# Attention scores from two fp32r parts in 64-row halves, with TensorE's order in a group written out by hand

## What is computed

```
qkv = x @ w_attn.T;  q, k = rope(q), rope(k)
scores = q @ k.T / sqrt(16), masked above the diagonal
y = softmax(scores) @ v + gating * softmax(q @ ak.T / sqrt(512)) @ av
x = layernorm(x + y @ w_proj.T)
base = x @ base_w.T + base_b;  res = x @ A.T;  probs = softmax(x @ router_w.T)
combine = top-2 of probs, normalised
x = layernorm(x + base + 0.5 * sum_e combine_e * (res @ B_e.T))
```

## Time and profile before

| | |
|---|---|
| median of 3 runs | 961.23 us (957.89 to 962.98) |
| profiled execution, its own time | 958.21 us |
| its span in the trace | 956.5 us |
| TensorE busy | 885.7 us, 93% of the span |
| VectorE busy | 737.3 us, 77% |
| ScalarE busy | 496.7 us, 52% |
| stage A, about | 0 to 233 us |
| stage B, about | 233 to 699 us |
| stage C, about | 699 to 956 us |

### The profile page before, as it was taken

The page is one execution under the profiler, slowest core; times in us unless marked ns, Lnnn a source line. Parts: engine busy times, 40 slices in busy tenths (PEclk is TensorE's granted clock), DMA queues, the critical chain, the costliest instruction groups (busy, mean ns, idle before and its releaser), DMA issues.

```text
span 956.5 us, 16144 instructions
## 1 busy us (share of the span) xinstructions
PE 885.7 (93%) x5420; PEld 493.3 (52%) x5420; DVE 737.3 (77%) x2225; ACT 496.7 (52%) x1052; POOL 259.3 (27%) x285
## 2 busy tenths in 40 slices
PE   5999999886999999999999999999978999999996
PEld 4878787561223222332222333222357888888884
DVE  4676757769898889888889988887555777767766
ACT  4243434232777777777777788778751122121210
POOL 0324334222232322332322332223331221212211
PEclk9999999985999999999999999999989999999999
DMA  7224143316555433455533455436110101011010
GB/s 248 55 68 121 56 122 98 95 30 134 101 99 101 100 62 61 81 100 101 94 60 62 87 100 100 86 63 180 47 34 1 36 31 44 22 44 35 31 34 33
DMA packets 50410, 73.11 MB, mean 76 GB/s; under 512 B 8996, under 2 KB 21540, under 8 KB 50340
## 3 DMA queue, kind: packets, MB, share of 16 engines
q1 hardware_dynamic: 49828, 71.43, 32.4%
q10 hardware_dynamic: 512, 0.79, 0.3%
HBM read 55.12 MB, written 16.78 MB: 75 GB/s over the span
## 4 chain that ended last, share of the span: by engine, by line
PE 78%; DVE 12%; ACT 6%; issue 2%; DMA 1%; POOL 1%; SPq 0%; DVEq 0%; ACTq 0%
PE bank L1328 17%; PE bank L1427 15%; PE bank L1338 10%; PE bank L385 10%; PE bank L386 9%; PE bank L387 9%; PE bank L1528 4%; ACT pt L790 3%; PE bank L1409 1%; DVE xl L872 1%; DVE xtl L1058 1%; ACT xth L815 1%; DVE asb L933 1%; DVE asum L936 1%; ACT asb L694 1%
## 5 line engine op out<-in xcount | busy, mean ns | idle before, releaser
L790 ACT ACTIVATE pt<-bank 128x512 f32<-128x512 f32 (+3 forms) x768 | 334.1, 493 | 96.3 <-PE bank L1328 88.7
L955 DVE CUSTOM_DVE_ANT_0 bank<-bank,cmask 128x512 f32<-128x512 f32 (+3 forms) x512 | 234.8, 523 | 24.5 <-PE bank L1338 22.7
L1328 PE MATMUL bank<-qs,ks 98*128 98x512 bf16 (+3 forms) x768 | 208.1, 335 | 19.0 <-ACT pt L790 18.9
L958 DVE TENSOR_REDUCE mx<-bank 128x1 f32<-128x512 f32 x256 | 163.4, 685 | 31.8 <-PE bank L1338 31.6
L620 POOL TENSOR_SCALAR_AFFINE_SELECT pt<-pt 128x512 f32<-128x512 f32 x128 | 83.6, 653 | 327.8 <-ACT pt L790 327.8
L1427 PE MATMUL bank<-pt,vb 128*32 128x512 f32 (+3 forms) x1536 | 164.5, 500 | 0.9 <-POOL pt L620 0.9
L1328 PEld LDWEIGHTS bank<-qs,ks 98*128 98x128 bf16 x768 | 57.8, 97 | 179.2 <-ACT pt L790 131.6
L1338 PE MATMUL bank<-km,qm 48*128 48x512 bf16 (+3 forms) x768 | 124.0, 340 | 11.4 <-DVE mx L955 7.8
L1338 PEld LDWEIGHTS bank<-km,qm 48*128 48x128 bf16 x768 | 32.6, 94 | 119.6 <-DVE mx L958 42.2
L815 ACT CAST xth<-bank 128x512 fp32r<-128x512 f32 x16 | 9.4, 586 | 146.2 <-PE bank L1502 146.2
L955 DVE DVE_READ_ACCUMULATOR2_ANT mx<- 128x1 f32 x512 | 72.3, 141 | 0.0
(11 more groups left out here) (152 smaller groups left out, 1435.6 us busy)
## 6 DMA issues: line engine op xcount, KB each, us to landing
qs<-q_parts SPq DMA_DIRECT2D x32, 256.0 KB
q_parts<-part SPq DMA_DIRECT2D x48, 128.0 KB, 2.4
k_parts<-part SPq DMA_DIRECT2D x48, 128.0 KB, 2.4
ks<-k_parts SPq DMA_DIRECT2D x16, 384.0 KB
qs<-q_parts SPq DMA_DIRECT2D x32, 128.0 KB
ks<-k_parts SPq DMA_DIRECT2D x16, 256.0 KB
qm<-in_x SPq DMA_DIRECT2D x16, 256.0 KB, 2.7
out<-outb SPq DMA_DIRECT2D x16, 256.0 KB, 2.0
```

The source lines that it names most:

```text
L790: act.activation(pt[k % PT_BUFS][:, h, 0:width(st)], half(n % SCORE_BUFS)[:, 0:width(st)], ACT.Exp, scale=float(HD) ** -0.5).then_inc(S("e ...
L955: last = ve.tensor_tensor_reduce(blk, blk, cmask[:, BANK - nk * P:], 1.0, NEG, ALU.add, ALU.max, mx[m][:, 0, h, qt:qt + 1])
L958: last = ve.tensor_reduce(mx[m][:, 1, h, qt:qt + 1], blk, AX.X, ALU.max)
L1328: pe.matmul(half(n % SCORE_BUFS)[:, 0:q1 - q0], ks[g % 2][0:KX, h, kb * P:(kb + 1) * P], qs[g % 2][0:KX, h, q0:q1], start=True, stop=True) ...
```

## The change

- q and k are split in two parts, both fp32r (4 bytes), instead of three bf16 parts (`PARTS` 2). `second` and the second subtraction on GpSimd go; GpSimd's one subtraction writes the low part. The stores are 4 DMAs for a unit instead of 6.
- Maxima and scores use the same three terms (48 rows) and the same buffers: `qm` and `km` are gone, `qs` and `ks` are three each, laid out in halves, heads 0 and 2 of a group on partitions from 0, heads 1 and 3 from 64. A score contracts over 50 rows (`KX`), from partition `64 * (h % 2)`.
- SyncE loads a group once, two groups ahead (`load_group`, 8 DMAs); the rows of maxima go in two DMAs instead of one, and the ones in six instead of two. The load of group 1 stands later than that of its maxima did, after all values of the last tile.
- The places of V, of the copies, of the pairs of maxima and of the transposes are tables of numbers. `LEAD` is 8 instead of 10, `ROWS_LAG` 2 instead of 4.
- Stage C: other buffers hold the same tiles; `bias` has its own semaphore, and VectorE waits for `rev_ld` alone. In `ve_c`, `lo_y(2)` goes ahead of `low_b(2)`, `low_b(3)` behind `lo_x(1)`, and `lo_g(0)` ahead of `norms(2)`. The first tiles' y and projection stand at other places of the last group.

```diff
-PARTS = 3
-TERMS = [(0, 0), (0, 1), (0, 2), (1, 0), (1, 1), (2, 0)]
+PARTS = 2
+TERMS = [(0, 0), (1, 0), (0, 1)]
 KR = len(TERMS) * HD
 KX = KR + 2
-LEAD = 10
-ROWS_LAG = 4
+LEAD = 8
+ROWS_LAG = 2
+VALUES_AT = [13, 17, 19, 22, 26, 33, 37, 42, 44, 48, 51, 57]
+PAIRS_AT = [0, 2, 6, 7, 11, 13, 16, 18, 22, 23, 26, 28, 31, 33, 37, 41, 42, 46]
...
-            qs[i] = sb(bc, f"qs{i}", [P, HG, T], BF16)
+            qs[i] = sb(bc, f"qs{i}", [P, 2, T], F32R)
...
+            def load_group(g):
+                if g >= 3:
+                    sp.wait_ge(S("score_full"), SCORE_BANKS * (g - 2))
+                issue_group(sp, g)
...
+            def remainder(tau, j):
+                gp.wait_ge(S("part_high"), 4 * tau + j + 1)
+                gp.tensor_tensor(part[j % 2][:, 1], rope[j % 2][:], part[j % 2][:, 0], ALU.subtract).then_inc(S("part_low"), 1)
...
-            ve.wait_ge(S("cc_ld"), 32)
+            ve.wait_ge(S("rev_ld"), 16)
...
                 if not sure and j == 1:
+                    lo_y(2, 0)
                     low_b(2)
+                if not sure and j == 2:
+                    low_b(3)
...
+                r0 = HALF * (h % 2)
+                pe.matmul(half(n % SCORE_BUFS)[:, 0:q1 - q0], ks[g % 3][r0:r0 + KX, h // 2, kb * P:(kb + 1) * P],
+                          qs[g % 3][r0:r0 + KX, h // 2, q0:q1], start=True, stop=True).then_inc(S("score_full"), 1)
```

More of the change, by code:

```diff
@@ L114 @@
 SLOTS = NMX + 3
-NORM_CHUNK = [COPY_AT[1] - SCORE_BANKS + 5, COPY_AT[0] + 5]
-NORM_OF = [(-1, 1), (0, 0)]
 def place_slots():
-    read = [sum(nk * P + READ_START for _, _, nk in max_of((LEAD + n) % NMX)[2]) for n in range(NMX)]
-    all_read, all_exps = sum(read) + ROWS_COLUMNS, sum(EXPS[:SCORE_BANKS]) + 4 * (BANK + READ_START)
-    first, norm_at, rows_at, tiles, slot, done, exp = [], [], None, 0, 0, 0, 0
+    first, norm_at, calc_at, rows_at, slot, tiles = [], [], None, None, 0, 0
     for c in range(SCORE_BANKS):
@@ L130, in place_slots @@
             norm_at.append(slot)
-            slot, exp = slot + 1, exp + BANK + READ_START
-        while tiles < NMX and done * all_exps <= exp * all_read:
-            if rows_at is None and tiles == NMX - LEAD + ROWS_LAG:
-                rows_at = slot
[L135 to L145, removed]
+            slot += 1
+        for _ in range(PAIRS_AT.count(c)):
+            if tiles == NMX - LEAD:
+                calc_at = slot
+            if tiles == NMX - LEAD + ROWS_LAG:
+                rows_at = slot
+                slot += 1
+            slot, tiles = slot + 2, tiles + 2
+    assert slot == SLOTS and tiles == NMX
+    return first + [SLOTS], norm_at, calc_at, rows_at
+FIRST, NORM_AT, CALC_AT, ROWS_AT = place_slots()
 def max_tile(slot):
@@ L198, with runs @@
 EARLY = (16, 26)
[L202 to L203 removed]
+Y_AT = [5, 7]
+PROJ_AT = [(11, 12, 15, 16), (21, 24, 25, 29)]
 Y_BANK, PROJ_BANK, X_BANK, ROUTER_BANK, FF_BANK = 3, 4, 5, 2, (7, 6)
 CW = [("w_projT", 0), ("base_wT", 0), ("B_T", 0), ("B_T", CC)]
[L212 to L217, removed]
+def runs(pick):
     out, r = [], 0
[L220 removed]
+    while r < len(TERMS):
         n = 1
[L222 removed]
+        while r + n < len(TERMS) and TERMS[r + n][pick] == TERMS[r + n - 1][pick] + 1:
             n += 1
[L224 removed]
+        out.append((r, n, TERMS[r][pick]))
         r += n
     return out
[L229 to L230 removed]
+LOADS = 2 * (len(runs(0)) + len(runs(1)))
 def drive_tiles(eng, step):
@@ L274, in build @@
             rope = [sb(a, f"rope{i}", [P, 2, TT]) for i in range(2)]
-            rem = sb(a, "rem", [P, 2, TT])
+            rtmp = [sb(a, f"rtmp{i}", [P, TT]) for i in range(2)]
             xh, xl = [None, None], [None, None]
@@ L739, in _ @@
                         x_high(tau + 1, 1 - u, 1)
-                    second(tau, 2)
                     if tau == TILES - 1:
@@ L1209, in ve_c @@
                 if not sure and j == 1:
-                    low_b(3)
+                    invert(G - 1, 1)
+                if not sure and j == 2:
+                    lo_g(0)
                 if sure or j >= 2:
                     norms(j, m)
-                if not sure and j == 2:
-                    lo_g(0)
-                if sure or 1 <= j < NTC - 1:
+                if sure or 2 <= j < NTC - 1:
                     lo_y(j + 1, 1 - m)
-                if not sure and j == 1:
-                    invert(G - 1, 1)
             drive_tiles(ve, ve_c)
```

191 lines of the change are left out of this document (73 added, 118 removed).

## The result

The changed kernel took **923.62 us** (median of 4 runs, 920.50 to 924.77) against 960.63 us for the kernel before (4 runs, 957.89 to 962.98): ratio 0.961, 95% interval 0.9575 to 0.9646. Forecast were 920.0 us and 899 to 947. The profiled execution took 920.5 us, span 918.8. The time lies 4 us from the forecast. The reasons behind it are for the most part wrong, as the experiments show, and errors of both signs cancelled.

A forecast was written before the change was run, and what follows sets the result against it. The prediction took TensorE's queue to bound stage B. Gains of 29.4 (14 periods), 0.7 (last group), 2.5 (seam) and 7.0 (head of stage C) sum to 39.6 us; 958.21 became 918.6, given as 920.0, range 899 to 947.

The forecast's parts named there:

- TensorE's queue bounds the group: Stage B of the kernel before: TensorE busy 27.70 of 28.90 us in a group, VectorE 25.75.
- 27 x 0.11 = 3.0 us go: TensorE in a group: 27 changes of height between maxima and scores, 0.11 us each, disappear, saving 3.0 us.
- 12 x 0.1: TensorE in a group: fp32r weight loads lie open at 12 exits from V, costing 0.1 us each.
- Overlap of scores: TensorE in a group: scores in different halves stream side by side; 60% of a possible 4.4 us, 2.6 us, is gained.
- No pairing, only better placing of the pairs: Low end of the period's gain: 0.4 us a group, out of TensorE's 1.2 us wait.
- Rival 1: Stage B: pairs do not overlap or tables buy less; TensorE stays the bound at about 28.2; 938 to 945 us, chance 0.17.
- VectorE becomes the leader, and the period cannot go under 25.75: Stage B: TensorE's work falls to about 25.1 us, under VectorE's 25.75; period 26.8, gain 2.1 us.
- VectorE busy over 95% of a group: Stage B: sign named to show the forecast right, beside a V step 0 period of about 26.8 us.
- Last group, +0.7: Between group 14 and the end: 1.8 us lost to new height changes against up to 4.4 from pairs; gain 0.7 us.
- Seam, 2.5 gained: From stage A to B: k is stored earlier with one cast and one subtraction gone; net gain 2.5 us, ends 0 and 4.
- Head of stage C, 7.0: Start of stage C: three TensorE waits, 8.0 us, go; `lo_x(1)` may come 0.8 late; net gain 7.0 us.
- 903 to 935 from its ends: Whole kernel: the forecast's own range, from the ends of its terms, without the rivals; the forecast itself had chance 0.60.

## Why the prediction came out right, point by point

The number came out by luck: the mechanism of the period was wrong, and the stretches ahead of the periods and behind them came out with the wrong sign.

- *"TensorE's queue bounds the group" in the kernel before*: right.
- *"Counting the order, 27 x 0.11 = 3.0 us go", and fp32r's cost sums to the same, net 0.0*: about right. On the new tables the halves are worth 27.05 - 26.11 = 0.94 us a period; less the 0.8 of overlap, 0.1 to 0.2 is left. The single terms were off. Added up from start to start over a period on the new tables, the steps among scores and maxima take 12.5 us with bf16 parts and 10.1 with halves, overlap included. Entering the twelve V steps costs 0.8 more, the transposes 0.7 more. Leaving V costs nothing more (0.52 us at 512 columns in both), where I had put 12 x 0.1. And the new order would have 33 changes of height with bf16 parts, not the 27 of the old one that I counted. (What follows a maximum after 0.32 us in the earlier trace rows is an fp32r matmul of full height, not a score; the earlier trace rows have the score after 0.33.)
- *Overlap of scores, "I take 60%, 2.6 us"*: the mechanism exists, the size was three times too big. In a period of the changed kernel, 8 of 19 steps from one score to the next are under 0.03 us, and 11 of 32 between a score and a maximum. Why the rest do not overlap was not tested; that ScalarE frees the banks one by one is my guess.
- *"No pairing, only better placing of the pairs" as the low end, 0.4 us*: the step that failed. I priced the tables at no more than part of TensorE's 1.2 us wait and took none of it; they gave 1.85 us a period, 26 of the 39 us. I read the waits by their idle time, where the records hide up to 0.17 of each, and I looked at pairs only, not at the V places, which are the larger part. Rival 1 failed in the same way: it gave the tables 0.7 us.
- *"VectorE becomes the leader, and the period cannot go under 25.75"*: false as a mechanism, though the period came to 26.11. With 3.5 us less on VectorE it was 26.05. The sign that I had named, VectorE busy over 95% of a group, came true (97%) and proved nothing.
- *Last group, +0.7 from "16 x 0.11 = 1.8 us lost" against pairs*: wrong sign. A passage to full height and back costs 0.39 more than with 98-row bf16 scores, where I had 2 x 0.11, hence 8 x 0.39 = 3.1 us, and scores between projections find no partner, which was not measured apart. In an execution without low clock there (the head set back) the stretch took 42.0 us against 37.2 with bf16 parts: 4.8 lost; the stall of 1.3 us behind VectorE is a part of it. The Trainium skill ("TensorEngine Tiling (Array Packing)", Key Properties) has the change of tiling mode drain the engine; the trace agrees that such changes cost, by 0.2 us each here with fp32r operands.
- *Seam, 2.5 gained*: wrong sign for the stretch, though the wait that I priced did go: ScalarE's 2.0 us for the stored k in group 0 are in the trace of the kernel before and not in that of the changed one. But stage A ended later: the last rotation began at 231.1 us against 226.4, and the first exponential of group 0 at 237.4 against 234.1, where I had said 236 for that of the third step. Of these 4.7 us, 0.6 had come by 157 us, with the three waits for `x_low` (5.4 against 4.7 us); 1.6 came at once behind 3.4 us at half clock at 155 to 158 us, which the kernel before did not have; 2.5 came later, among the maxima of the last tile, which at half clock start 0.78 us apart instead of 0.70. That fp32r makes these slower is argued. In every execution with halves the last rotation began at 227.9 us or later, in every one with bf16 parts by 226.5. The prediction called stage A's steps hidden.
- *Head of stage C, 7.0*: right in its mechanism, measured 9.7. Of the waits that I listed the second went, 0.66 and 0.23 us stayed of the first and the third, and what came late next was `lo_x(1)`, 1.19 us against the 0.8 I gave: 8.0 - 2.1 = 5.9 us. The other 3.8 us are not waits of the list. The granted clock was 0.83 from 700 to 720 us and 0.91 to 0.92 from 720 to 740 us in the kernel before and 1.00 there in the changed one; that is up to 5 us, an estimate, and luck.
- *Range, 899 to 947*: its terms do not give it. The ends of the four terms add up to 898 and 950 us; the "903 to 935 from its ends" follows from nothing shown.
- The sum held by luck: the two ends came out 14 us worse than forecast (11 lost, 3 forecast as gain), the periods and the head of stage C 12 us better.

## What to carry to other kernels

Where one engine's queue is strictly in order and feeds two others, price the order first: change the tables alone before the operands, and test an engine that looks 97% full by taking work from it. An operand format that is cheap beside its own kind can cost at each passage to the other kind, so count the passages in the stages that only border on the change, and put the pieces of the other kind together. A chain that is mended locally (a stall of 1.8 us, three times) is worth nothing until one has seen which load or clock comes late next.

## What the runs showed of the hardware

**fp32r at half height went with longer spells of low clock.** At the seam, TensorE waits much for VectorE, and the granted clock falls to 0.50, that is 1.2 GHz, in every kernel. It came back at different times, though TensorE was busy nearly throughout. The stretch from 240 to 280 us, first before, then the changed kernel with the head set back, then halves with the old order (from 260 on):

```profile
240.00:250.00 10.00, 9.66 (x66) 2.92 (x66) 7.43 (x29) 7.02 (x19) 2.47 (x4) 0.82 1.01 185
250.00:260.00 10.00, 9.49 (x73) 2.64 (x72) 9.36 (x34) 7.81 (x17) 2.59 (x4) 1.00 0.26 54
```

```profile
240.00:250.00 10.00, 10.00 (x54) 4.73 (x52) 7.65 (x27) 5.51 (x13) 2.47 (x4) 0.50 0.83 157
250.00:260.00 10.00, 9.66 (x59) 4.74 (x57) 7.92 (x20) 6.60 (x16) 1.27 (x2) 0.67 0.01 2
260.00:270.00 10.00, 10.00 (x50) 3.92 (x51) 5.57 (x26) 5.49 (x11) 1.96 (x3) 0.54 0.01 4
```

```profile
260.00:270.00 10.00, 9.48 (x47) 4.21 (x43) 6.56 (x25) 4.98 (x12) 2.29 (x4) 0.50 0.00 1
270.00:280.00 10.00, 10.00 (x45) 3.66 (x44) 5.76 (x17) 4.73 (x9) 0.93 (x2) 0.51 0.14 38
```

The price in the second of these is a first full period of 30.5 instead of 26.1 us. Of eleven profiled executions with halves, six had a first full period 2.6 to 6.8 us too long for their tables; of three with bf16 parts none, but the one with the new head spent 38 us at 0.50 at the seam, as long as the changed kernel's own, and paid ahead of that period. In all, the spell at the seam lasted 27, 31 and 38 us with bf16 parts and 34 to 61 with halves; the mean granted clock was 0.966 to 0.978 in all recorded executions with bf16 parts and 0.909 to 0.978 with halves. The one with the old order also had two periods of 36.40 and 35.85 us late in stage B, with 37 us at 0.50 in them, after ten at full clock. Executions of one kernel differ by this: with the old V places 949.7 us at a mean granted clock of 0.977, and 961.6 at 0.960. So the ranges overlap, and three executions are few. What brings a spell on, and whether halves prolong it or only go with it, stays open; I had no run that separates the type from the height.

**A subtraction on GpSimd held up the one on VectorE beside it.** GpSimd's 128x1024 subtraction took 2.14 us before and 2.39 in the changed kernel; VectorE's 1.22 us subtraction beside it took 2.31 and 2.54. It ended 1.1 us behind GpSimd's both times (63.15 against 62.06 us, 63.28 against 62.21), as if it had done nearly all of its work after that. Run with GpSimd's behind it, it took 1.22. GpSimd's second operand was bf16 before and is fp32r now, and its output f32 and now fp32r, so whether reading or writing made it slower is not separated.
